# The attention probabilities of two units of every later row turned by DVE and two DMA hops instead of by TensorE

## What is computed

```python
h = _layernorm(x, norm1_g, norm1_b)
h = _neighborhood_attn(h, qkv_w, qkv_b, proj_w, proj_b)
x = shortcut + h
m = _layernorm(x, norm2_g, norm2_b)
m = jax.nn.gelu(m @ fc1_w + fc1_b, approximate=False) @ fc2_w + fc2_b
return x + m
...
main = jax.nn.gelu(x @ W1m + b1m) @ W2m + b2m
probs = jax.nn.softmax(logits, axis=-1)
top_vals, top_idx = lax.top_k(probs, K)
expert_out = jnp.einsum('bk,bknd->bnd', gate_w, eo)
return a * main + (1.0 - a) * expert_out
...
scores = jnp.einsum('bld,blwd->blw', q, kw) / scale
attn = jax.nn.softmax(scores, axis=-1)
out = jnp.einsum('blw,blwd->bld', attn, vw)
```

## Time and profile before

| | |
|---|---|
| timed runs | 1855.82 and 1856.29 us, median 1856.05 |
| the profiled execution | 1854.73 us, its span 1852.9 us |
| busy in the span | PE 1840.6 us (99%), DVE 1371.1 (74%), ACT 1167.8 (63%), POOL 870.9 (47%) |
| instructions | PE 19591, DVE 2226, ACT 1832, POOL 788 |
| granted clock of PE | 1.0 |

### The profile page before, as it was taken

One profiled execution on the slowest core, in us unless ns is written; L12 is line 12 of the kernel. 1 busy time (PEld: TensorE's weight loads), 2 busy tenths in 40 slices (PEclk: granted clock), 3 DMA queues, 4 the chain that ended last, 5 costly groups with the idle time before them and its releaser, 6 DMA issues.

```text
span 1852.9 us, 49302 instructions
## 1 busy us (share of the span) xinstructions
PE 1840.6 (99%) x19591; PEld 1664.4 (90%) x19591; DVE 1371.1 (74%) x2226; ACT 1167.8 (63%) x1832; POOL 870.9 (47%) x788
## 2 busy tenths in 40 slices
PE   8999999999999999999999999999999999999999
PEld 7899898998989989899898999989899898998998
DVE  7777877778777686776868777787777877778644
ACT  6775756657566575665756657566576755657554
POOL 6555271553716437163462624536255271552725
PEclk9999999999999999999999999999999999999999
DMA  4231312203122031220313113131131311203121
GB/s 144 63 91 31 98 58 52 75 30 98 58 69 69 20 104 53 83 61 24 98 46 92 53 34 93 41 97 54 39 89 34 97 58 51 77 29 98 47 64 58
DMA packets 147437, 121.88 MB, mean 66 GB/s; under 512 B 17964, under 2 KB 139784, under 8 KB 147208
## 3 DMA queue, kind: packets, MB, share of 16 engines
q1 hardware_dynamic: 146512, 117.90, 21.9%
q10 hardware_dynamic: 696, 0.83, 0.1%
HBM read 85.52 MB, written 8.39 MB: 51 GB/s over the span
## 4 chain that ended last, share of the span: by engine, by line
PE 97%; DVE 1%; DMA 0%; ACT 0%; issue 0%; POOL 0%; ACTq 0%; DVEq 0%; POOLq 0%
PE psB L261 58%; PE psA L261 28%; PE psA L1272 4%; PE psA L1289 3%; PE psA L1161 2%; PE psA L1311 2%; DMA raw<-in_L_attn_qkv_w 0%; PE psA L1327 0%; DVE smax L745 0%; POOL wf_lo L513 0%; DVE smax L732 0%; DMA xin<-in_L_attn_x 0%; DVE pr L749 0%; ACT hr_hi L988 0%; ACT pT L992 0%
## 5 line engine op out<-in xcount | busy, mean ns | idle before, releaser
L632 DVE TENSOR_TENSOR hr_lo<-hf,hr_hi 128x512 fp32r<-128x512 f32 x512 | 507.4, 991 | 401.4 <-ACT hr_hi L988 401.3
L522 POOL TENSOR_SCALAR chosen_w<-raw 128x512 fp32r<-128x512 f32 x256 | 197.8, 773 | 644.5 <-DMA raw<-in_L_ffn_W2e 385.4
L988 ACT ACTIVATE hr_hi<-hf 128x512 fp32r<-128x512 f32 x512 | 323.9, 633 | 261.7 <-PE psB L261 179.7
L524 POOL TENSOR_TENSOR chosen_w<-raw,chosen_w 128x512 fp32r<-128x512 f32 x256 | 409.0, 1597 | 21.3
L261 PE MATMUL psB<-z_hi,chosen_w 128*128 128x512 f32 x1024 | 371.5, 404 | 0.0
L261 PE MATMUL psB<-chosen_w,hr_hi 128*128 128x256 f32 x2032 | 360.6, 277 | 0.3 <-DVE hr_lo L632 0.2
L261 PEld LDWEIGHTS psB<-chosen_w,hr_hi 128*128 128x128 f32 x2032 | 322.8, 188 | 19.4 <-DVE hr_lo L632 1.0
L984 ACT ACTIVATE hf<-psB,b1x 128x512 f32<-128x512 f32 x256 | 175.1, 684 | 174.6 <-PE psB L261 173.4
L261 PE MATMUL psB<-chosen_w,hr_lo 128*128 128x256 f32 x1016 | 282.1, 278 | 0.0
L261 PEld LDWEIGHTS psB<-z_hi,chosen_w 128*128 128x128 f32 x1024 | 192.3, 188 | 36.0
L261 PE MATMUL psB<-z_lo,chosen_w 128*128 128x512 f32 x512 | 200.1, 391 | 0.0
(11 more groups left out here) (207 smaller groups left out, 4247.7 us busy)
## 6 DMA issues: line engine op xcount, KB each, us to landing
raw<-in_L_ffn_W1e SPq DMA_DIRECT2D x256, 128.0 KB, 2.2
raw<-in_L_ffn_W2e SPq DMA_DIRECT2D x256, 128.0 KB, 2.2
vb<-vs SPq DMA_DIRECT2D x64, 192.0 KB
vb<-vs SPq DMA_DIRECT2D x64, 160.0 KB
out_x<-acc SPq DMA_DIRECT2D x31, 256.0 KB, 2.2
xin<-in_L_attn_x SPq DMA_DIRECT2D x15, 512.0 KB, 3.8
tm<-in_L_ffn_b2e SPq DMA_DIRECT2D x32, 128.0 KB, 3.0
raw<-in_L_attn_fc_w SPq DMA_DIRECT2D x8, 256.0 KB, 3.9
```

The costliest lines, as they stand in the source:

```text
L522: g.tensor_scalar(wx[0][:, :, s, :], raw[:, s, :].rearrange("p (a n) -> p a n", a=2), 1.0, 0.0, ALU.mult, ALU.add).then_inc(w_hi.sem, 1)
L524: g.tensor_tensor(wx[1][:, :, s, :], raw[:, s, :].rearrange("p (a n) -> p a n", a=2), wx[0][:, :, s, :].bitcast(f32), ALU.subtract).then_i ...
L632: v.tensor_tensor(hr[1][:, c % 2, :], hf[:, c % 3, :], hr[0][:, c % 2, :].bitcast(f32), ALU.subtract).then_inc(h_lo.sem, 1)
L988: a.activation(hr[0][:, c % 2, :], hf[:, c % 3, :], ACT.Copy).then_inc(h_hi.sem, 1)
```

## The change

In rows 1 to 15 units 0 and 2 are no longer transposed by PE and copied by ACT. DVE turns their probabilities in blocks of 32x32 in one instruction of 128x1024 (`turn_blocks`), into `y` for unit 0 and `sx` for unit 2, directly after normalise(0) at step 3, and at step 9 ahead of normalise(3). The blocks are then in the wrong partitions. SP writes all of them, 512 KB, to a scratch tensor in device memory, waits for that to land, and reads them back into `pT` with four DMAs of 128 KB, one for each group of 32 partitions (`place_blocks`); for unit 0 ahead of load 5, for unit 2 ahead of load 8. attend(0) and attend(2) wait for these reads. Units 1 and 3 are turned as before.

Some work moves: the queries of unit 2 are placed by ACT at step 3 instead of DVE; norm1_y goes from step 5 to step 6 behind `turned(1)` and also waits for the first write to the scratch tensor, because it writes `y`; norm1_bias goes from step 7 to 8. Waits on PE's transposes become waits on the DVE transposes (`mask`) or on the masks (`scores`, `turn`).

```diff
+    SQ = 32
+    LANDED = (0, 2)
...
+        blocks_out = nc.dram_tensor("blocks_out", [len(LANDED), HS, P, UB * QB], f32, kind="Internal").ap()
...
+        def blocks(u):
+            return (sx if u else y)[:, :, :].rearrange("p i n -> p (i n)").rearrange("p (c b k) -> p c b k", c=HS, k=SQ)
+
+        def turned_block(t, u, b, s):
+
+            if t and u in LANDED:
+                return pT[:, :, :].rearrange("p b q -> p (b q)")[0:PK, (s * UB + b) * QB:(s * UB + b + 1) * QB]
+            return turned_unit(t, u)[0:PK, b, QB * s:QB * s + QB]
...
+            def place_blocks(t, u):
+
+                i = LANDED.index(u)
+                sp.wait_ge(blk_s.sem, blk_s.at(t - 1, i))
+                if u:
+                    sp.wait_ge(av.sem, av.at(t, 1))
+                else:
+                    sp.wait_ge(t1_lo.sem, t1_lo.all(t))
+                    sp.wait_ge(av.sem, av.all(t - 1))
+                sp.dma_start(blocks_out[i, :, :, :].rearrange("c p n -> p c n"), blocks(u).rearrange("p c b k -> p c (b k)")).then_inc(blk_out.sem, 16)
+                sp.wait_ge(blk_out.sem, blk_out.at(t - 1, i))
+                for c in range(HS):
+                    dst = pT[SQ * c:SQ * c + SQ, :, :].rearrange("p b q -> p (b q)").rearrange("p (s n) -> p s n", s=HS)
+                    sp.dma_start(dst, blocks_out[i, c, :, :].rearrange("(s k) n -> k s n", k=SQ)).then_inc(pT_in[i].sem, 16)
...
+                            elif n == RING + 1 and 0 < t < ROWS:
+                                place_blocks(t, 0)
+                            elif n == 2 * RING and 0 < t < ROWS:
+                                place_blocks(t, 2)
...
-                    elif q == 7 and t:
+                    elif q == 8 and t:
                         norm1_bias(t)
...
+            def turn_blocks(t, u):
+
+                v.wait_ge(normed.sem, normed.at(t, u))
+                if u:
+                    v.wait_ge(acc_s.sem, acc_s.at(t - 1, 1))
+                else:
+                    v.wait_ge(sx_s.sem, sx_s.at(t - 1))
+                v.transpose(blocks(u), pr[:, 0, :, :, :].rearrange("p b (h g) k -> p b (h g k)", h=1).rearrange("p b (c k) -> p c b k", k=SQ)).then_inc(blk_s.sem, 1)
...
                         if q == 3:
                             normalise(t, 0)
+                            if t:
+                                turn_blocks(t, 0)
                         elif q == 9:
+                            if t:
+                                turn_blocks(t, 2)
                             normalise(t, 3)
...
-                    elif q == 3 and t < ROWS:
-                        if t:
-                            query_blocks(t, 2)
-                        else:
-                            normalise(t, 1)
-                            shifts(t)
+                    elif q == 3 and t == 0:
+                        normalise(t, 1)
+                        shifts(t)
...
             def norm1_y(t):
                 if t:
                     a.wait_ge(sx_s.sem, sx_s.at(t - 1))
+                    a.wait_ge(blk_out.sem, blk_out.at(t - 1, 0))
...
                     elif q == 3 and t:
                         keys(t, 1)
+                        query_blocks_first(t, 1)
                     elif q == 4:
-                        turned(t, 0)
                         if t:
                             query_blocks(t, 3)
                         else:
+                            turned(t, 0)
                             exp(t, 2)
-                    elif q == 5 and t:
-                        norm1_y(t)
                     elif q == 6:
                         turned(t, 1)
                         if t == 0:
                             exp(t, 3)
-                            norm1_y(t)
+                        norm1_y(t)
...
                     elif q == 10:
-                        turned(t, 2 if t else 3)
+                        if t == 0:
+                            turned(t, 3)
...
+                if t and u in LANDED:
+                    pe.wait_ge(pT_in[LANDED.index(u)].sem, pT_in[LANDED.index(u)].all(t - 1))
...
-                    elif q == 4:
+                    elif q == 4 and t == 0:
                         turn(t, 0)
-                        if t == 0:
-                            scores(t, 2)
+                        scores(t, 2)
...
-                    elif q == 10:
-                        turn(t, 2 if t else 3)
+                    elif q == 10 and t == 0:
+                        turn(t, 3)
```

More of the change, by code:

```diff
@@ L245, in build @@
         normed, trp, pT_s, av = signal("normed", 4), signal("trp", 8), signal("pT", 8), signal("av", 8)
+        blk_s, blk_out = signal("blk", len(LANDED)), signal("blk_out", len(LANDED), 16)
+        pT_in = [signal(f"pT_in{u}", HS, 16) for u in LANDED]
         tA_hi, tA_lo, proj = signal("tA_hi", KD), signal("tA_lo", KD), signal("proj", 2)
@@ L282, in turned_unit, with turn_value @@
             return (acc if t else sx)[:, :, :].rearrange("p i n -> p (i n)").rearrange("p (b q) -> p b q", q=P)
+        def turn_value(t, u, h):
+            by_pe = [n for n in range(4) if n not in LANDED]
+            return 2 * u + h + 1 if t == 0 else 8 + 2 * len(by_pe) * (t - 1) + 2 * by_pe.index(u) + h + 1
+        def blocks(u):
[4 more added lines that the diff above has]
+            return turned_unit(t, u)[0:PK, b, QB * s:QB * s + QB]
         def unit_scores(t, u):
@@ L714, in mask @@
                     v.wait_ge(score.sem, score.at(t, u))
-                    if u >= 2:
-                        v.wait_ge(trp.sem, trp.at(t, 2 * (u - 2) + 1))
+                    if u - 2 in LANDED:
+                        v.wait_ge(blk_s.sem, blk_s.at(t - 1, LANDED.index(u - 2)))
+                    elif u >= 2:
+                        v.wait_ge(trp.sem, turn_value(t, u - 2, 1))
                     elif t:
@@ L1042, in turned @@
                 for h in range(2):
-                    a.wait_ge(trp.sem, trp.at(t, 2 * u + h))
+                    a.wait_ge(trp.sem, turn_value(t, u, h))
                     if t > 1 and u == 1:
@@ L1046, in turned @@
                     elif t and u == 3:
-                        a.wait_ge(trp.sem, trp.at(t, 5))
+                        a.wait_ge(blk_s.sem, blk_s.at(t - 1, LANDED.index(2)))
                     elif u > 1:
@@ L1261, in scores @@
                     pe.wait_ge(masked.sem, masked.at(t - 1, 1))
+                elif u > 1 and t and u - 2 in LANDED:
+                    pe.wait_ge(masked.sem, masked.at(t - 1, 2 * u - 1))
                 elif u > 1 and t:
-                    pe.wait_ge(pT_s.sem, pT_s.at(t, 2 * (u - 2) + 1))
+                    pe.wait_ge(pT_s.sem, turn_value(t, u - 2, 1))
                 for b in range(UB):
@@ L1280, in turn @@
                         if u:
-                            pe.wait_ge(pT_s.sem, pT_s.at(t, 2 * (u - 1) + h))
+                            pe.wait_ge(pT_s.sem, turn_value(t, u - 1, h))
                         else:
@@ L1286, in turn @@
                     else:
-                        pe.wait_ge(pT_s.sem, pT_s.at(t, 4 + h))
+                        pe.wait_ge(masked.sem, masked.at(t - 1, 6 + h))
                     for j in range(4):
@@ L1298, in attend @@
                     pe.wait_ge(qm_odd.sem, qm_odd.all(t))
+                if t and u in LANDED:
+                    pe.wait_ge(pT_in[LANDED.index(u)].sem, pT_in[LANDED.index(u)].all(t - 1))
                 for h in range(2):
-                    pe.wait_ge(pT_s.sem, pT_s.at(t, 2 * u + h))
+                    if t == 0 or u not in LANDED:
+                        pe.wait_ge(pT_s.sem, turn_value(t, u, h))
                     for j in range(4):
@@ L1310, in attend @@
                             w = (HS * c + s) * G * HD
-                            last = pe.matmul(psA[cols, 2 + c, at:at + QB], vb[0:PK, j, 2 * th + h, w:w + G * HD], turned_unit(t, u)[0:PK, b, cols], start=True, stop=True)
+                            last = pe.matmul(psA[cols, 2 + c, at:at + QB], vb[0:PK, j, 2 * th + h, w:w + G * HD], turned_block(t, u, b, s), start=True, stop=True)
                     last.then_inc(av.sem, 1)
@@ L1448, in _ @@
                         for c in range(KD):
-                            pe.wait_ge(pT_s.sem, pT_s.at(t, 6 + c))
+                            pe.wait_ge(pT_s.sem, turn_value(t, 3, c))
                             transposes(tr2, c, tm, c)
```

## The result

The changed kernel took 1890.03 and 1890.29 us, median 1890.16, against 1856.05 before: ratio 1.0186, interval 1.0170 to 1.0202. That is 34.1 us slower, where 14 us had been forecast. The sign was right, and step 11 was the main place; the size was off by 20 us. The time lies within the range that was given (1846 to 1893), but that is luck: the upper end was built from a transpose of 2.32 us and a d of 0.4 us in every row, and the runs showed neither.

A forecast was written before the change was run, and what follows sets the result against it. PE was taken as the bound (busy 99%), with DVE's train equally late at step 11. The transpose's 1.15 us there outweighed PE's saving: 0.91 us x 15 = 13.7 us, 1870 us; bounds 1858 to 1892, range 1846 to 1893.

The forecast's parts named there:

- a transpose of 2.32 us: DVE, step 9: upper end for unit 2's added transpose, giving 2.0 us a row, 1886 us.
- d: Shift of ACT's train that leads to DVE: -0.2 to 0 us, taken as 0; 0.4 if the first write lands late, adding 6 us.
- PE, removed: 16 of 32 transposes a row go from PE: 0.87 us per unit, 1.74 us per row, 26.1 us in 15 rows.
- 2.65: PE's predicted wait in us at step 11, from wanting to start down(9) at 1030.17 until h_low(9) ends at 1032.82.
- the sum is even: ACT: two pairs of PSUM copies go (1.07 us a pair), four query blocks come from DVE (1.93 us).
- I take 1.15: DVE, step 9: unit 2's transpose delays h_low(9) by its whole length, 1.15 us, ends 0.69 and 2.32.
- 0.91: Predicted lateness in us of PE's start of down(9) at step 11, per row, against before.
- part of the gain stays: Rival: h_low(9) loses 0.41 us and the train follows PE by 0.87, step 11 0.37 us early per row, 1850 us; chance 0.17.
- The small rest: PE's clock falls in its new waits; with PE idle for 1.83 us it had stayed at 1.00; rest given 0.05.
- The two hops: Unit 2's write and reads take 7.4 us of 8.27, costing nothing; rival that they are late: 1911 us at 11 us, chance 0.15.
- The sum: At step 11 down(9) starts 0.91 us late per row, x 15 = 13.7 us, 1870 us in all.

The follow-up runs named there:

- the transpose alone: The kernel before with one DVE transpose of unit 2 added between gather and normalise(3), its result not used: 1880.38 us, ratio 1.0136.
- the filled wait: The changed kernel with eight unused matmuls added on PE ahead of down(9) in each row from 1 on: 1881.40 us, ratio 1.0139 to the kernel before.
- unit 2 alone: The changed kernel with the change for unit 2 only, all of unit 0 as before the change: 1890.25 us, ratio 1.0194 to the kernel before.
- the split later: The kernel before with the unused DVE transpose of unit 2, and POOL's split of load 4 waiting for h_low(9): 1870.38 us, ratio 1.0082.

## Why the prediction was wrong in size

- *PE, removed.* Right: scores(1) to attend(0), which holds one unit's transposes, is 0.40 us shorter net in row 11, 0.87 without the wait at turn(1), and turn(2) gives another 0.87. But the first unit's saving is not all lost at step 11, as the prediction had it; half goes at turn(1), behind DVE's mask(2), and some more at down(8). PE therefore comes to step 11 about 1.1 us early and not 1.74, and waits 2.38 us from start to start, as the prediction counted its 2.65 (2.23 us of idle time). Its busy time fell by 5 us only and not by 26 to 31; the half clock in 7 rows is part of that.
- *ACT.* d was 0 in row 11, as taken. The first write took 3.2 to 4.6 us to land, where 2.2 to 3.8 had been allowed, and y waited for it in 5 rows (3.0 us in all, up to 1.1); these rows are longer by about as much, some 3 us of the total. The other move, of unit 2's query blocks to step 3, was not looked at for its place: "the sum is even", but hr_hi(4) and all that follows it on DVE up to mask(2) came later, by 0.96 us at hr_hi(4) and 0.45 at mask(2). That this is what makes PE wait at turn(1) is read from the trace of row 11; no run tests it by itself.
- *DVE, the step that failed.* "I take 1.15" was right for the transpose itself (1.17 on the path). The 2.5 us estimated from the Trainium skill, VectorE: DVE Perf Modes, "The three transpose paths", does not agree with the 1.246 us of the trace. The step priced one instruction and left its neighbours as the earlier trace rows have them. In row 11 there come 0.19 for the wait on gather's end and 0.60 for the multiply that now meets POOL's subtraction, and 0.42 goes from h_low(9): 0.91 becomes 1.30 at the start of down(9), and 0.1 more for its first matmuls (0.51 us where the earlier trace rows have 0.41). The row is 1.40 us longer. (In the kernel with the transpose alone it is 1.65; POOL's subtraction begins 0.18 us later against DVE there, and the multiply takes 1.77.) The 0.41 that the rival "part of the gain stays" let vanish did vanish; it came back elsewhere on the same engine, larger.
- *The clock, the other step that failed.* "The small rest", set aside by one stretch of 1.83 us of idle time with the clock at 1.00, shorter than the wait of 2.65 that the prediction itself forecast. In waits of 2.23 us it fell to 0.50 in 7 rows of 15. It cost 8.0 to 8.8 us by the filled wait, 9.9 by the difference of unit 2 alone and the transpose alone.
- *The two hops.* Right: in row 11 the write is issued 0.02 us behind the transpose's end, the reads 2.93 us later, the last of the four 1.33 behind the first, and with 2.61 for that to land 6.9 us come out; over the 15 rows it is 6.8 to 8.1, median 7.5, against 7.4 forecast. The hand-overs, put at some 0.2 us each, took 0.02 to 0.03 where the trace shows them. The 4.8 us estimated for the reads from the 189 GB/s of the Trainium skill, SBUF — State Buffer, "Door 1: The DMA port swizzle", was too much; 3.9 was measured. Nobody waited. That held because PE was late, which the prediction said.
- *The sum.* 1.40 us x 15 = 21, seven falls of the clock at 1.5 = 10.5, y's waits 3: 34.5, measured 34.1. Of the 20 us that the forecast missed, about 7 are DVE's neighbours, 8 to 10 the clock and 3 the late write. All three terms are read from the changed kernel's own trace; the tests of the first two are the kernels with the transpose alone, the split later and the wait filled.

What decides which rows fall stays open: the same wait of 2.23 us left the clock at 1.00 in 8 rows of either kernel.

## What to carry to other kernels

An instruction put into a train without gaps moves everything behind it against the other engines; price its neighbours anew, above all two-input instructions that may now meet one of GpSimd, and not its own length alone. The same holds for what is moved to an engine that seems to have room. Work taken from PE ahead of a place where PE waits only makes that wait longer, and a longer wait can cost the clock as well: here 26 us of PE's work were taken away, and the kernel became 34 us slower. Look first for what needs the moved result soonest: with h_low(9), normalise(3), y, turn(3) and the later attends in other places, the same change was 13 us faster than the kernel before.

## What the runs showed of the hardware

- A two-input instruction of DVE and one of POOL did not run side by side. The multiply of 128x768 took 0.96 us alone, 1.56 or 1.77 us beside POOL's subtraction, according to how late POOL had begun; the sums and reciprocals ahead of it ran beside POOL at 0.91 and 0.25 us, as they did without POOL in the kernel with the split later.
- DVE's transpose of 128x1024 in float32 took 1.245 us for either destination, close to the 1.23 that the prediction carried over from the earlier trace rows; the two-input instruction of that size in the earlier trace rows takes 2.32.
- PE's granted clock fell in 7 of 15 waits of 2.23 us, in none of 15 of 1.37 us, and was back soon: 0.50 from 1052 to 1055 us in row 9, 0.95 from 1055 to 1058.
- Four reads of 128 KB, each onto 32 partitions, issued in 1.76 us, landed 2.5 us after their issue (median), close to the loads onto 128 partitions (2.3).
